# Two mixture-of-experts layers, each written as one block instead of four

## The reference, cut to what matters

```python
# layer 1: 8 experts, hidden 1024, one pick per row
expert_idx = argmax(softmax(x @ gate_w.T)); expert_w = its probability
out = sum_e where(expert_idx == e, (relu(x @ w1[e] + b1[e]) @ w2[e] + b2[e]) * expert_w, 0)

# layer 2: 16 experts in 4 groups, hidden 256, four picks per row from the two best groups
scores = sigmoid(x @ router_w.T); s = scores + bias      # bias decides the picks only
y_e = (silu(x @ gate_w[e]) * (x @ up_w[e])) @ down_w[e]
routed = sum over the 4 picks of y_e * 2.5 * score / sum(scores of the picks)
sh = (silu(x @ sh_gate_w) * (x @ sh_up_w)) @ sh_down_w   # shared expert, hidden 512, all rows
out = routed + sh
```

## Time and profile before

| | |
|---|---|
| median of 3 runs | 1816.34 us (1816.02 to 1816.98) |
| the profiled execution | 1812.46 us |
| its span, first to last instruction | 1810.7 us |
| busy: PE / PEld / DVE / ACT / POOL | 1375.2 / 1159.9 / 977.8 / 684.9 / 363.1 us |
| mean granted TensorE clock | 0.865 |
| layer 1's experts in the span | 444.0 to 687.5 us |
| layer 2's experts in the span | 1062.0 to 1456.2 us |

### The profile page before, as it was taken

How to read it: one execution, slowest core, us unless ns; L and a number is a source line. 1 busy time by engine, 2 the same in 40 slices (tenths; PEclk the granted TensorE clock), 3 DMA queues, 4 the chain that set the end, 5 groups by cost and what they waited for, 6 DMA issues and landing times. The chain is left out here.

```text
span 1810.7 us, 32769 instructions
## 1 busy us (share of the span) xinstructions
PE 1375.2 (76%) x10700; PEld 1159.9 (64%) x10709; DVE 977.8 (54%) x2405; ACT 684.9 (38%) x1355; POOL 363.1 (20%) x452
## 2 busy tenths in 40 slices
PE   4999657768699965999999979899998951102464
PEld 3777535667599964888877868599997941101232
DVE  3777654646422225555555546422222735888785
ACT  2555442500344411333333323355553252402454
POOL 1000000012122210222222223266664300001000
PEclk9999867889599997999999979699998986555787
DMA  3000020751211116111111020122222414120001
GB/s 95 19 17 13 16 70 1 242 203 24 68 36 35 32 37 197 59 44 43 43 43 43 1 79 4 36 93 90 93 91 77 173 57 109 13 56 1 0 0 47
DMA packets 96893, 108.65 MB, mean 60 GB/s; under 512 B 27888, under 2 KB 83952, under 8 KB 96496
## 3 DMA queue, kind: packets, MB, share of 16 engines
q1 hardware_dynamic: 84240, 79.35, 14.5%
q0 software_dynamic: 9984, 27.28, 4.8%
q10 hardware_dynamic: 2592, 1.05, 0.2%
HBM read 85.55 MB, written 20.97 MB: 59 GB/s over the span
## 5 line engine op out<-in xcount | busy, mean ns | idle before, releaser
L3452 PEld LDWEIGHTS L2f_bank<-L2f_xT,L2f_w_tile 128*128 128x128 f32 x1280 | 157.6, 194 | 4.0
L3452 PE MATMUL L2f_bank<-L2f_xT,L2f_w_tile 128*128 128x128 f32 x1280 | 158.0, 277 | 0.0
L758 POOL TENSOR_TENSOR L2x_probs<-L2x_probs,L2x_inv_sum 128x512 f32<-128x512 f32 x64 | 65.3, 1041 | 288.2 <-DVE L2x_inv_sum L1025 288.2
L3528 DVE TENSOR_TENSOR L2f_hT<-L2f_gate_h,L2f_bank 128x256 f32<-128x256 f32 x80 | 33.7, 421 | 151.9 <-ACT L2f_gate_h L3498 151.9
L3485 ACT COPY L2f_w_tile<-L2f_w_up 128x1024 f32 x80 | 83.7, 1047 | 45.6 <-issue 35.2
L3452 PEld LDWEIGHTS L1f_bank<-L1f_xT,L1f_w_tile 128*128 128x128 f32 x768 | 90.8, 194 | 1.1
L3452 PE MATMUL L1f_bank<-L1f_xT,L1f_w_tile 128*128 128x128 f32 x768 | 90.9, 277 | 0.0
L3390 POOL DMA_INDIRECT L2f_y_rows<-L2f_xn,L2f_put_row x80 | 79.2, 990 | 55.9 <-DVE L2f_xn L3544 52.7
L3382 POOL DMA_INDIRECT L2f_rows<-L2f_x_rows,L2f_take_row x80 | 77.8, 972 | 49.3 <-SPq L135 23.9
L3469 PE MATMUL L1f_bank<-L1f_w_down,L1f_hT 128*128 x384 | 86.7, 379 | 0.0
L1007 DVE TENSOR_REDUCE L2x_top<-L2x_bank 128x4 f32<-128x512 f32 x64 | 43.9, 686 | 79.0 <-PE L2x_bank L827 79.0
(11 more groups left out here) (652 smaller groups left out, 3379.4 us busy)
## 6 DMA issues: line engine op xcount, KB each, us to landing
L1f_w_up<-in_L_ffn_w SPq DMA_DIRECT2D x16, 512.0 KB, 10.2
L1f_w_down<-in_L_ffn_w SPq DMA_DIRECT2D x16, 512.0 KB, 9.9
L2f_got<-L2f_y_rows SPq DMA_DIRECT2D x16, 512.0 KB, 4.1
L2f_w_up<-in_L_ffn_gate_w SPq DMA_DIRECT2D x16, 256.0 KB, 2.9
L2f_w_up<-in_L_ffn_up_w SPq DMA_DIRECT2D x16, 256.0 KB, 3.2
L2f_w_down<-in_L_ffn_down_w SPq DMA_DIRECT2D x16, 256.0 KB, 3.6
x<-in_x SPq DMA_DIRECT2D x4, 512.0 KB, 7.6
L0x_ctx<-in_ctx SPq DMA_DIRECT2D x16, 128.0 KB, 2.1
```

Of the source, the lines that this page charges most:

```text
L758: nc.gpsimd.tensor_tensor(probs[c][:, :, :], probs[c][:, :, :], inv_sum[:, c, :][:, :, None].to_broadcast([P, 4, P]), ALU.mult).then_inc(s ...
L3452: x = nc.tensor.matmul(products(j, m), w_tile[j][:, at:at + P], xT[j][:, k * P:(k + 1) * P], start=(k == 0), stop=(k == KT - 1))
L3528: nc.vector.tensor_tensor(hT[j][:, 0:F], gate_h[j][:, 0:F], bank[2 + j][:, F:2 * F], ALU.mult).then_inc(q["h"], 1)
```

## The change

- Each layer's `routed_experts` is one block; the three inner meetings are gone. New waits stand in their place: `expert`, `taken` and `put` (counters of the DVE results that others read), `sh_w`, `b2` and `consts`. SP itself waits for all scatters ahead of the `got` loads.
- `ExpertLoads.rest`, called at the end of the SP list of the attention functions, loads router, router bias and `b1`.
- ACT issues the three loads of the shared expert's weights between its copies of batches 1 to 3.
- POOL fills `columns` and `tiles_no` after four batches are normalised.
- In layer 2 ACT takes the sigmoid of each batch's logits from PSUM; DVE's logits copies stay in layer 1 only. The logits move from banks 2 and 3 to banks 6 and 7.
- Ahead of the one-hot products PE does five fronts and four backs of the shared expert, and ACT four results (`EARLY = 6`). Back 4 and front 5 stand behind the one-hot products, back 5 behind the first tile's expansion, batches 6 to 15 behind the tile loop.
- The pick shares (`per_pick` on `share`) stand behind `put_row`.
- Some temporaries share memory with `w_tile` and `rows`.

The core of the diff:

```diff
@@ attention functions, SP
+            ahead.rest(sp)
@@ class ExpertLoads
+    def rest(self, sp):
+        ins, loaded, E = self.core.ins, self.sems["ahead"], self.spec["experts"]
+        for k in range(KT):
+            sp.dma_start(self.router[:, k, :], ins[self.spec["router"]][:, k * P:(k + 1) * P].rearrange("e p -> p e"),
+                         allow_slow_non_contiguous=True).then_inc(loaded, 16)
+        if self.gated:
+            sp.dma_start(self.bias[:, :], ins["L2_ffn_bias"].rearrange("(a n) -> a n", a=1).to_broadcast([P, E])
+                         ).then_inc(loaded, 16)
+        else:
+            sp.dma_start(self.b1[:, :], ins["L1_ffn_b1"].rearrange("e (m p) -> p (e m)", p=P),
+                         allow_slow_non_contiguous=True).then_inc(loaded, 16)
...
@@ routed_experts
-    EARLY = 7
+    EARLY = 6
...
+            pool.wait_ge(s["xn"], 4)
+            nc.gpsimd.iota(columns[:, :, :], [[1, P], [0, G]], 0, 0, allow_small_or_imprecise_dtypes=True
+                           ).then_inc(s["consts"], 1)
+            nc.gpsimd.iota(tiles_no[:, :, :], [[1, S], [0, G]], 0, 0, allow_small_or_imprecise_dtypes=True
+                           ).then_inc(s["consts"], 1)
...
-            pe.wait_ge(s["router"], 48 if gated else 32)
...
             finish_norm_scalar(core, act, s, temps)
+            take_T(0)
+            for b in range(B):
+                if b + 1 < B:
+                    take_T(b + 1)
+                if gated and b in (1, 2):
+                    act.dma_start(sh_gu[:, b - 1, :, :], ins[("L2_ffn_sh_gate_w", "L2_ffn_sh_up_w")[b - 1]]
+                                  .rearrange("(k p) f -> p k f", p=P)).then_inc(s["sh_w"], 16)
+                if gated and b == 3:
+                    act.dma_start(sh_down[:, :, :], ins["L2_ffn_sh_down_w"].rearrange("(m p) d -> p m d", p=P)
+                                  ).then_inc(s["sh_w"], 16)
+                if gated:
+
+                    act.wait_ge(s["logits"], b + 1)
+                    nc.scalar.activation(cols(abc[1], b * E, E), bank[6 + b % 2][:, 0:E], ACT.Sigmoid
+                                         ).then_inc(s["logits_out"], 1)
...
+            if gated:
+
+                pe.wait_ge(s["sh_w"], 48)
+                shared_front(pe, 0)
+                pe.wait_ge(s["logits_out"], B)
+                for b in range(EARLY - 2):
+                    shared_front(pe, b + 1)
+                    shared_back(pe, b)
+                    if b == 1:
+                        count_rows()
+            else:
+                count_rows()
             for n in range(PICKS // G):
 
                 pe.wait_ge(m["is_row"], n + 1)
...
+            if gated:
+                shared_activate(act, 0)
+                for b in range(EARLY - 2):
+                    shared_activate(act, b + 1)
+                    shared_result(act, b)
...
-            nc.vector.tensor_copy(put_row[:, :], target)
-
-
-        phases.close()
+            nc.vector.tensor_copy(put_row[:, :], target).then_inc(m["put"], 1)
+
+            for k in range(K):
+                per_pick(k, pick_share[:, k * B:(k + 1) * B], share)
...
@@ POOL
+            pool.wait_ge(m["taken"], 1)
             for t in range(4):
                 gather(t)
+            if gated:
+                shared_gated(pool, EARLY - 1)
+                shared_added(pool, EARLY - 2)
             for t in range(S + LAG):
...
+                if gated and t == 1:
+                    shared_added(pool, EARLY - 1)
+                if t == LAG:
+
+                    pool.wait_ge(m["put"], 1)
                 if t >= LAG:
                     scatter(t - LAG)
 
-            for j in range(4):
-                pool.wait_ge(q[f"stored{j}"], 16 * S // 4)
+            if gated:
+                shared_gated(pool, EARLY)
+                for b in range(EARLY, B):
+                    if b + 1 < B:
+                        shared_gated(pool, b + 1)
+                    shared_added(pool, b)
...
@@ PE
+            if gated:
+                shared_back(pe, EARLY - 2)
+                shared_front(pe, EARLY - 1)
+
+            pe.wait_ge(m["expert"], 1)
             transposed(0, 0)
+
+            pe.wait_ge(m["put"], 1)
             transposed(1, 1)
             expand(0, 0)
+            if gated:
+                shared_back(pe, EARLY - 1)
             transposed(2, 2)
+            if gated:
+                pe.wait_ge(c["down_out"], EARLY)
             over_tiles(pe, body, S)
+            if gated:
+
+                pe.wait_ge(q["h"], S)
+                shared_front(pe, EARLY)
+
+                pe.wait_ge(q["y"], S)
+                for b in range(EARLY, B):
+                    if b + 1 < B:
+                        shared_front(pe, b + 1)
+                    shared_back(pe, b)
...
@@ ACT
+            if gated:
+                shared_result(act, EARLY - 2)
+                shared_activate(act, EARLY - 1)
+
+            act.wait_ge(m["expert"], 1)
             place_weights(0, 0)
             take_T(0, 0)
             take_T(1, 1)
             place_weights(1, 1)
+            if gated:
+                shared_result(act, EARLY - 1)
             activate(0, 0)
...
@@ SP
+            for j in range(4):
+                sp.wait_ge(q[f"stored{j}"], 16 * S // 4)
             for b in range(B):
 
                 after(sp, g["added"], 2 * K * (b // 2 - 1))
```

More of the change, by code:

```diff
@@ new lines, in shared_front @@
+        def shared_front(pe, b):
+            j = b % 2
+            after(pe, c["up_out"], b - 1)
+            for u in range(2):
+                for f in range(SH // P):
+                    for k in range(KT):
+                        t = nc.tensor.matmul(bank[2 + 2 * j + u][:, f * P:(f + 1) * P],
+                                             sh_gu[:, u, k, f * P:(f + 1) * P], xT_of(b)[:, k * P:(k + 1) * P],
+                                             start=(k == 0), stop=(k == KT - 1))
+            t.then_inc(c["up"], 1)
@@ new lines, in shared_back, with shared_activate @@
+        def shared_back(pe, b):
+            j = b % 2
+            pe.wait_ge(c["h"], b + 1)
+            after(pe, c["down_out"], b - 1)
+            for f in range(SH // P):
+                t = nc.tensor.matmul(bank[6 + j][:, 0:D], hT[j][:, f * P:(f + 1) * P], sh_down[:, f, :],
+                                     start=(f == 0), stop=(f == SH // P - 1))
+            t.then_inc(c["down"], 1)
+        def shared_activate(act, b):
+            j = b % 2
+            act.wait_ge(c["up"], b + 1)
+            after(act, c["h"], b - 1)
+            nc.scalar.activation(gate_h[j][:, :], bank[2 + 2 * j][:, :], ACT.Silu)
+            nc.scalar.copy(up_h[j][:, :], bank[3 + 2 * j][:, :]).then_inc(c["up_out"], 1)
@@ L3258, in _ @@
                                      ).then_inc(m["own"], 1)
+        if gated:
+            @block.gpsimd
+            def _(pool):
+                shared_gated(pool, 0)
+                for b in range(EARLY - 2):
+                    shared_gated(pool, b + 1)
+                    shared_added(pool, b)
         @block.vector
@@ L3549, in _ @@
             if not gated:
-                dve.wait_ge(s["extra"], 16 * n_extra)
+                dve.wait_ge(s["b2"], 16)
+            dve.wait_ge(m["expert"], 1)
             front(0, 0)
             over_tiles(dve, body, S)
-        late = list(range(EARLY, B)) if gated else []
-        g = core.sems_in(f"{tag}g", (SHARED_SEMS if gated else []) + [f"got{j}" for j in range(4)] + ["added"])
-        block = phases.open()
         @block.sync
         def _(sp):
+            for j in range(4):
+                sp.wait_ge(q[f"stored{j}"], 16 * S // 4)
             for b in range(B):
@@ L3567, in _ @@
                              ).then_inc(g[f"got{b % 4}"], 16)
-        if gated:
-            shared_expert(block, g, late)
         @block.vector
```

216 lines of the change are left out of this document (78 added, 138 removed).

## The result

The changed kernel takes 1796.18 us, median of four runs (1792.48 to 1796.96), against 1816.18 for the kernel before beside it (1814.19 to 1816.98): ratio 0.9889, 95% interval 0.9874 to 0.9905, some 20 us faster. The forecast was 30, to 1786.3, at least 1779 and at most 1796.

A forecast was written before the change was run, and what follows sets the result against it. TensorE was taken to bound the kernel, with gains only where it stands still outside the tile loop. Layer 1's 10.3 us (6.15 + 4.2) and layer 2's 19.7 (15.8 + 3.9) make 30.0: median 1786.3, range 1779 to 1796.

The forecast's parts named there:

- (a): Expert stages' heads: iota moved back, loads moved into the attention stage at no cost; first transpose 2.6 us (layer 2), 1.1 (layer 1) earlier.
- Heads: Starts of both expert stages: layer 2's counting products 4.6 us earlier; layer 1 gains 1.1 at first transpose, 2.5 at fifth normalise.
- Loads from ScalarE: Layer 2's head: shared weights, loaded from ScalarE, run beside the x_rows stores; charged 0.2 us (0 to 2).
- One-hot rows: Layer 2: ScalarE has only four shared results ahead of them, so TensorE's one-hot products end 16.8 us earlier, at unchanged length.
- Into the loop: Layer 2, one-hot products to expand(1): gather covered by shared work, expand(1) 15.3 us earlier, and 0.5 for full clock: 15.8.
- Layer 1 into the loop: Layer 1's start of the tile loop: 6.15 us earlier, from head gains 1.1 and 2.5, 0.6, and 1.95 between take_row and gather.
- Behind the loops: After the tile loops, without the DRAIN's meeting: layer 1's combination gains 4.2 us, layer 2's end a net 3.9.
- Rival 2: The DRAIN's cost is the scatters' own work, so SP waits as long; layer 1 loses 4.0 us: 1790.3. Chance 0.10.
- rival 1: Heads and joints give little: iotas 2.5 us, stores 2, ScalarE's chain 2.5, DRAIN 1.2 lost, 8.2 in all: 1794.5. Chance 0.15.
- Rival 3: More than forecast: TensorE keeps its clock through the joints, 1.6 + 1.5 + 1.5 us: 1781.7. Chance 0.12.
- rival 4: Tile loop: GpSimd or gathers set the pace and each tile gets longer; at 3.3 us a tile, 1821. Chance 0.03.
- rival 5: The change does not overlap what it says; layer 2's 15.8 us falls to 5: 1797. Chance 0.07.

The follow-up runs named there:

- e1: The changed kernel with layer 1's moved router and expert bias loads issued behind the attention stage's inner meeting: 1783.98 us against 1814.97 for the kernel before.
- e5: The changed kernel with the 1024- and 640-column iotas of both expert layers back among GpSimd's first operations: 1794.55 us, ratio 0.9884 to the kernel before.
- e8: The changed kernel with the first two tiles' expert weight copies ahead of ScalarE's shared work before the tile loop: 1790.99 us, ratio 0.9861 to the kernel before.
- e6: The changed kernel with a new block, so a meeting of all engines, between layer 1's tile loop and its combination: 1798.76 us, ratio 0.9919 to the kernel before.
- e9: The changed kernel with layer 1's router and expert biases loaded in its expert stage again, first transpose waiting for the biases too: 1791.38 us, ratio 0.9873.
- e12: The changed kernel with layer 1's router and biases loaded in its expert stage, first transpose waiting for the router alone: 1821.71 us against 1847.76 for the kernel before.

## Why the prediction was wrong

**The step that failed** is in (a): "With the loads gone into the attention stage (whose SP queue is done long before its end; I cost them there at nothing, 0 to 3 us if they were late)". It was not done long before what mattered. The stage's end is 66 us behind SP's last issue, but its inner meeting is where SP ends: SP's last issue in the kernel before ended at 378.25, VectorE passed at 378.71. The step held SP's last issue against the stage's end and did not ask who ended the 11 us wait in its middle. The term is 10 us (e1 against the runs with L1x as changed: 118.3 against 128.3 to 128.5; 11.8 in the profiled run, in whose second block the clock was reduced for longer, 0.77 instead of 0.81 in its first 31.4 us). Its largest allowance was 3, and none of the rivals had it. The rest of the sum was 2.1 us too large (27.9 for 30.0). With the loads behind the meeting (e1) the time is 1784.0, below the forecast in part by the chance named there.

**Heads.** Right. Layer 2: TensorE reaches the shared products 4.7 us earlier behind the start and the counting 4.0 (forecast 4.6); the 0.7 between them went to the first two fronts, 10.14 us instead of 9.42, at half clock for their first half. The first transpose came 1.9 and not 2.6 earlier, since beside GpSimd's operations that stayed in front one of the norm still lasts 0.92. Layer 1: 1.2 (1.1), and the fifth normalise lasts 1.79 beside the moved iotas, without a wait ahead of it. The port rule of the Trainium skill ("SBUF — State Buffer", Who interferes with whom) agrees with both: by e5 the stretch goes where the iota goes. Of TensorE's time it took 0.80 us ahead of layer 1's fifth transpose, where TensorE had waited 3.50 before: 2.7 gained, forecast 2.5.

**Loads from ScalarE.** The shared weights' transfers held the x_rows stores up (VectorE waits 4.09 us once), but with four buffers TensorE kept its 1.17 us a batch. The 0.2 stands. By the Trainium skill's rule of shared engines ("Trainium Kernel Development and Optimization", Key Constraints) the charge would have been 2. The 4.09 us fit the rule, which no run here tests; at TensorE it cost nothing.

**One-hot rows.** Right: 16.1 us earlier behind the start, forecast 16.8. They are as long as before, 18.73.

**Into the loop.** 15.3 forecast, 13.4 measured (expand(1) at 88.6 behind the start, 102.0 before). 0.7 is from above, 1.2 is this joint. expand(0) began 0.8 sooner behind the one-hot products than in my sum; from there to expand(1) it took 2.1 more, nearly all of it the lower clock, which I had in back(4) alone: expand(0) and back(5) took 2.95 and 2.70 where I set 2.0 and 1.7. e8 shows that one us less of waiting removes it. The 0.5 for full clock at expand(1) came (2.02 instead of 2.46).

**Layer 1 into the loop.** 5.3 of 6.15 at the last scatter: the gather came 0.9 behind take_row, not 0.2.

**Behind the loops.** Layer 1: scatter to load 2.5 us instead of 6.8, so 4.4 (forecast 4.2). Rival 2 falls by this row and by e6. Layer 2: 60.9 us from the last tile's product to layer 3's first norm instead of 65.0, so 4.1 (3.9). The ten batches' chain ends last, as said; GpSimd's clean-up ends at 1439.5, 4.5 us behind the end of its last addition (1434.97): it costs what it did, and its row of 5.25 begins with that addition. It ends 0.85 behind VectorE's last (1438.65). I charged 0.2 of at most 1.2.

**The rivals.** Of rival 1's four terms the DRAIN showed 0.85 and ScalarE's chain, with its clock, 1.2; the iotas took 0.80 us of TensorE in layer 1, the stores nothing. Rival 3's kept clock came only in e8. The loop takes 2.87 us a tile as before, so rival 4 had no part in it, and the overlap is there, against rival 5.

## What to carry to other kernels

A load is free only if the engine that issues it is not the last at the next meeting. Before work is put on a queue, look at the issue times: here 0.4 us was room and 2.2 us a full queue, and what was added there delayed the meeting by all of its issue time (9.5 us of rows, 10 of meeting). Look in each stage for who ends the long waits of all the others, also in stages that a change hardly touches; here that view was worth 8 us more than was asked.

## What was not expected of the hardware

Two 4 KB router loads, read element by element, hold SP for 6.3 us and the 32 KB of biases for 3.2 to 3.5 behind large loads; at a stage's start, on an idle queue, the same issues take 1.0 and 0.57 (e9). GpSimd's clean-up in a stage with indirect transfers lasts 4.0 us in layer 1 and 4.5 in layer 2, counted from the end of its last operation or of its wait for the scatters, in the kernel before and in the change alike, also where the last scatter lies 54 us back (layer 2, changed kernel). It can lie beside other engines' work when no meeting follows. On the chip of e12 the kernel before took 1847.76 us (there is no trace of it there) and e12's expert stage of layer 2 409.0, although TensorE's clock was 1.00 in the loop; in a 240 us stretch TensorE was busy 220.1, and at some of its gaps of about 0.5 us the trace shows nothing that it waited for. Layer 1's expert stage was not slower on that chip: take_row to the last scatter is 181.5 us, 181.7 in the change. Why was not tried.
